# Expert products of a routed feed-forward layer from rounded float32 halves: three products instead of one full float32 product

## The reference

```python
x = x + attention(layernorm(x), W_DKV, W_UK, W_UV, W_UQ, W_O)
xf = layernorm(x).reshape(-1, 256)               # 4096 tokens
topw, topi = top_k(xf @ Wr / temp, 2);  topw = softmax(topw)
for e in range(8):
    a, g = split(xf @ W1[e] + b1[e], 2)          # W1[e]: 256 x 1024
    y = a * silu(g) @ W2[e] + b2[e]              # W2[e]: 512 x 256
    out += y * (weight of expert e for the token, else 0)
x = x + out
```

## Time and profile before

| What | Value |
|---|---|
| median of three runs | 1242.43 us |
| profiled execution, first to last instruction | 1240.9 us |
| PE busy in it | 1069.9 us (86%) |
| DVE, ACT, POOL busy | 787.0, 491.9, 390.4 us |
| projection, attention, routing, expert phase, about | 0 to 126, 126 to 613, 613 to 806, 806 to 1241 us |
| DMA moved | 121.22 MB |

### The profile page before, as it was taken

How to read it: one execution, slowest core, us unless ns; L and a number is a source line. 1 busy time by engine, 2 the same in 40 slices (tenths; PEclk the granted TensorE clock), 3 DMA queues, 4 the chain that set the end, 5 groups by cost and what they waited for, 6 DMA issues and landing times. The chain is left out here.

```text
span 1240.9 us, 19607 instructions
## 1 busy us (share of the span) xinstructions
PE 1069.9 (86%) x5364; PEld 554.3 (45%) x5365; DVE 787.0 (63%) x2352; ACT 491.9 (40%) x1043; POOL 390.4 (31%) x721
## 2 busy tenths in 40 slices
PE   6897599999999999998587553089999999999995
PEld 2443123333333333332176543046666666666663
DVE  5654599999999999894057443245555555555553
ACT  2333047777777777777501212012122122122121
POOL 2224513333333333333403235512222222222222
PEclk9878569999999999999987565589999999999998
DMA  2665974444466644400266641212232232232232
GB/s 91 208 189 188 199 157 104 122 113 113 116 141 135 132 82 79 80 20 30 66 220 193 225 124 68 103 39 44 46 50 42 45 49 42 44 49 42 44 49 25
DMA packets 102396, 121.22 MB, mean 98 GB/s; under 512 B 26352, under 2 KB 81776, under 8 KB 102320
## 3 DMA queue, kind: packets, MB, share of 16 engines
q1 hardware_dynamic: 89024, 102.55, 32.5%
q0 software_dynamic: 13296, 17.77, 8.6%
HBM read 70.27 MB, written 49.63 MB: 97 GB/s over the span
## 5 line engine op out<-in xcount | busy, mean ns | idle before, releaser
L640 ACT ACTIVATE b_prob<-b_prob_ps 128x512 f32<-128x512 f32 (+3 forms) x768 | 318.0, 506 | 103.2 <-PE b_prob_ps L684 101.2
L596 DVE CUSTOM_DVE_ANT_0 b_max_ps<-b_max_ps,b_mask_max 128x384 f32<-128x384 f32 (+3 forms) x512 | 246.7, 503 | 50.4 <-PE b_max_ps L666 47.9
L666 PE MATMUL b_max_ps<-b_k_st,b_q_st 96*128 96x512 bf16 (+3 forms) x768 | 253.5, 345 | 24.2 <-DMA b_k_st<-k_parts 21.8
L684 PE MATMUL b_prob_ps<-b_q_st,b_k_st 99*128 99x512 bf16 (+3 forms) x768 | 239.5, 330 | 10.5 <-ACT b_prob L640 6.6
L554 POOL TENSOR_SCALAR_AFFINE_SELECT b_prob<-b_prob 128x128 f32<-128x128 f32 x512 | 146.6, 292 | 308.6 <-ACT b_prob L640 300.9
L1352 POOL DMA_INDIRECT out_dram<-e_y,e_token x71 | 110.1, 1551 | 326.1 <-DVE e_y L1406 310.4
L599 DVE TENSOR_REDUCE b_neg_max<-b_max_ps 128x1 f32<-128x512 f32 x256 | 176.1, 688 | 5.1 <-PE b_max_ps L666 2.6
L666 PEld LDWEIGHTS b_max_ps<-b_k_st,b_q_st 96*128 96x128 bf16 x768 | 74.4, 99 | 202.0 <-DVE b_neg_max L596 110.1
L703 PE MATMUL b_acc_ps<-b_prob,b_v_aug 128*32 128x512 f32 (+3 forms) x1536 | 163.4, 498 | 0.2 <-POOL b_prob L554 0.2
L1459 PE MATMUL e_g_ps<-w_sb,e_rowsT 128*128 x284 | 135.5, 600 | 0.3 <-issue 0.3
L1459 PE MATMUL e_a_ps<-w_sb,e_rowsT 128*128 x284 | 134.0, 594 | 0.0
(11 more groups left out here) (164 smaller groups left out, 1093.4 us busy)
## 6 DMA issues: line engine op xcount, KB each, us to landing
w_sb<-in_L_ffn_W SPq DMA_DIRECT2D x11, 1024.0 KB, 11.3
e_rows<-slot_rows SPq DMA_DIRECT2D x72, 129.0 KB, 2.1
ctx_cols<-b_ctx_out SPq DMA_DIRECT2D x16, 512.0 KB
q_parts<-a_part_q SPq DMA_DIRECT2D x8, 768.0 KB, 3.8
k_parts<-a_part_k SPq DMA_DIRECT2D x8, 768.0 KB, 4.2
b_q_st<-q_parts SPq DMA_DIRECT2D x16, 384.0 KB, 5.0
b_k_st<-k_parts SPq DMA_DIRECT2D x16, 384.0 KB, 7.7
a_x<-in_L_attn_x SPq DMA_DIRECT2D x8, 512.0 KB, 6.5
```

Source lines behind the costliest of these rows:

```text
L596: nc.vector.tensor_tensor_reduce(scores, scores, mask_max[:, HALF - width:HALF], -1.0, -MASKED, ALU.add, ALU.min, to).then_inc(max_done, 1)
L640: nc.scalar.activation(prob[n % NP][:, 0:width], prob_ps[n % NS][:, 0:width], ACT.Exp, scale=SCALE).then_inc(prob_ok, 1)
L666: nc.tensor.matmul(out[:, 0:width], q_st[g % RING][0:STACK, h, i * P:(i + 1) * P], k_st[g % RING][0:STACK, h, half * HALF:half * HALF + wi ...
L684: nc.tensor.matmul(prob_ps[n % NS][:, 0:width], k_st[g % RING][0:MAXROWS, h, j * P:(j + 1) * P], q_st[g % RING][0:MAXROWS, h, q0:q0 + widt ...
```

## The change

The expert products are no longer made from float32 operands. Each operand is split in two: a high part rounded to the type float32r (float32 words with a shortened mantissa), and a low part, the float32r of the difference. Each product is then three products of float32r operands, high x high, high x low, low x high, summed in PSUM.

*Weights.* In attention SP loads the weights of one expert at a time as they are (`b_w_raw`, 1.5 MB in two DMAs). POOL splits them in 12 pieces of 128 x 256 columns, a cast and a subtraction each, one piece after each of units 24e+8 to 24e+19. In loop step g = 2e+3 SP waits for the last piece of expert e, stores both parts to DRAM (two DMAs of 1.5 MB), and loads the next expert. In routing SP loads the parts of experts 0 to 3 from DRAM into a ring of four experts in SBUF, 3 MB per batch. In the expert phase SP loads expert e over expert e-4 as soon as the last tile of e-4 is done.

*Expert phase.* After each transpose ACT writes the high part, and DVE the low part. The weighting moves from DVE to ACT, the row loads from SP to ACT, the copy of the token numbers from DVE to POOL. B is 6, the loop has six steps, the results of a tile are taken one step later, and the table has one entry more.

The core of the diff:

```diff
-FC_EARLY = 3
+W1_COLS = DC * 2 * FF
+W_COLS = W1_COLS + FC * D
+W_RING = 4
+PIECE = 256
+PIECES = W_COLS // PIECE
...
+    SPLIT_UNITS = TOTAL // EXPERTS
+    SPLIT_FIRST = 8
...
+            def store_split(e):
+                sp.dma_start(dram["w_hi"][e], w_hi[:].bitcast(F32)).then_inc(split_st, 16)
+                sp.dma_start(dram["w_lo"][e], w_lo[:].bitcast(F32)).then_inc(split_st, 16)
...
             load(0)
             for g in range(NQUAD + 2):
                 if g + 1 < NQUAD:
                     load(g + 1)
-                if g < EXPERTS:
-                    sp.dma_start(w1_sb[:, g, :, :], w1[g].rearrange("(c p) n -> p c n", p=P)).then_inc(loaded, 16)
-                elif g < EXPERTS + FC_EARLY:
-                    f = g - EXPERTS
-                    sp.dma_start(w2_early[f][:], w2.rearrange("e (f p) n -> f p e n", p=P)[f]).then_inc(loaded, 16)
+                if g == 0:
+                    load_raw(0)
+                if g >= 3 and g % 2 == 1:
+                    e = (g - 3) // 2
+
+                    sp.wait_ge(lo_ok, PIECES * (e + 1))
+                    store_split(e)
+                    if e + 1 < EXPERTS:
+                        load_raw(e + 1)
                 if 0 <= g - 1 < NQUAD:
                     w = (g - 1) % RING
                     sp.wait_ge(rows_ok, g)
...
+            def split(e, k):
+
+                cols = slice(k * PIECE, (k + 1) * PIECE)
+                if k == 0:
+                    pool.wait_ge(raw_ok, 32 * (e + 1))
+                    if e:
+
+                        pool.wait_ge(split_st, 32 * e)
+                nc.gpsimd.tensor_copy(w_hi[:, cols], w_raw[:, cols]).then_inc(hi_ok, 1)
+                pool.wait_ge(hi_ok, e * PIECES + k + 1)
+                nc.gpsimd.tensor_tensor(w_lo[:, cols], w_raw[:, cols], w_hi[:, cols].bitcast(F32),
+                                        ALU.subtract).then_inc(lo_ok, 1)
...
-                for f in range(FC_EARLY, FC) if b == 0 else ():
-                    sp.dma_start(w2_sb[f][:], w2.rearrange("e (f p) n -> f p e n", p=P)[f]).then_inc(loaded, 16)
+                for part, of in zip(w_ring, (dram["w_hi"], dram["w_lo"])):
+                    sp.dma_start(part[:, b, :].bitcast(F32), of[b]).then_inc(w_in, 16)
...
+            sp.wait_ge(w_in, 32 * W_RING)
+            sp.sem_inc(w_ready, W_RING)
+            for e in range(W_RING, EXPERTS):
+
+                done = sp.value_load(tiles_done[0:1, e - W_RING:e - W_RING + 1], min_val=0, max_val=SLOT_TILES)
+                sp.wait_ge(y_ok, done + B)
+                for part, of in ((w_hi, dram["w_hi"]), (w_lo, dram["w_lo"])):
+                    sp.dma_start(part[:, e % W_RING, :].bitcast(F32), of[e]).then_inc(w_in, 16)
+                sp.wait_ge(w_in, 32 * (e + 1))
+                sp.sem_inc(w_ready, 1)
...
                 pool.wait_ge(y_ok, n + 1 + B)
+                pool.sem_inc(turn, 1)
+                nc.gpsimd.tensor_copy(token[c % B][:], rows[c % B][:, ROW_ID:ROW].bitcast(I32)).then_inc(token_ok, 1)
+                pool.wait_ge(token_ok, n + 1 + B)
                 pool.sem_inc(turn, 1)
                 nc.gpsimd.indirect_dma_start(
...
             def up(n, c, expert):
+                slot = expert % W_RING
+                pe.wait_ge(w_ready, expert + 1)
                 pe.wait_ge(rowsT_ok, n + 1)
...
+                        nc.tensor.matmul(out_ps[:], x_hi[:, chunk], moving(w_hi, slot, at, FF),
+                                         start=(d == 0), stop=False)
+                        nc.tensor.matmul(out_ps[:], x_hi[:, chunk], moving(w_lo, slot, at, FF),
+                                         start=False, stop=False)
+                        last = nc.tensor.matmul(out_ps[:], x_lo[:, chunk], moving(w_hi, slot, at, FF),
+                                                start=False, stop=(d == DC - 1))
```

More of the change, by code:

```diff
@@ L13 @@
 F32 = mybir.dt.float32
+F32R = mybir.dt.float32r
 BF16 = mybir.dt.bfloat16
@@ L556, in _ @@
                                                 channel_multiplier=-1).then_inc(causal_ok, 1)
+                e, k = divmod(unit, SPLIT_UNITS)
+                if SPLIT_FIRST <= k < SPLIT_FIRST + PIECES:
+                    split(e, k - SPLIT_FIRST)
         @block.vector
@@ L1277, in expert_phase @@
         hidden = [sb(f"e_hidden{n}", [P, FF]) for n in range(2)]
-        hiddenT = [sb(f"e_hiddenT{n}", [P, FF]) for n in range(2)]
+        hiddenT = [[sb(f"e_hiddenT_{part}{n}", [P, FF], F32R) for n in range(2)] for part in ("hi", "lo")]
         token = [sb(f"e_token{n}", [P, 1], I32) for n in range(B)]
@@ L1315, in steps @@
                     step(it * U + t, t, None)
-            for n in range(SLOT_TILES, SLOT_TILES + 2):
+            for n in range(SLOT_TILES, SLOT_TILES + tail):
                 step(n, n, n)
@@ L1326, in _ @@
         def _(sp):
-            def load(n, c):
-                row = sp.value_load(tile_row[0:1, n:n + 1] if isinstance(n, int) else tile_row[0:1, bass.ds(n, 1)],
-                                    min_val=0, max_val=EXPERTS * REGION + (SPARE - 1) * P)
-                sp.dma_start(rows[c % B][:], dram["rows"][bass.ds(row, P), :]).then_inc(rows_ok[c % B], 16)
-            for n in range(SLOT_LEAD + 1):
-                if n >= B:
-                    sp.wait_ge(y_ok, n + 1)
-                load(n, n)
-            with sp.Fori(0, LOOPS) as it:
-                for c in range(SLOT_LEAD, SLOT_LEAD + U):
-                    sp.wait_ge(y_ok, it * U + c + 2)
-                    load(it * U + c + 1, c + 1)
+            sp.wait_ge(w_in, 32 * W_RING)
[7 more added lines that the diff above has]
+                sp.sem_inc(w_ready, 1)
         @block.gpsimd
@@ L1424, in silu, with hidden_high, weighted @@
                 nc.scalar.activation(gate[c % 2][:], g_sum[c % 2][:], ACT.Silu).then_inc(gate_ok, 1)
-            def hidden_turned(n, c):
+            def hidden_high(n, c):
                 act.wait_ge(hiddenT_ps_ok, n + 1)
-                nc.scalar.activation(hiddenT[c % 2][:], hiddenT_ps[:], ACT.Copy).then_inc(hiddenT_ok, 1)
-            def step(n, c, value):
+                if not isinstance(n, int) or n >= 2:
+                    act.wait_ge(y_ps_ok, n - 1)
+                nc.scalar.activation(hiddenT[0][c % 2][:], hiddenT_ps[:], ACT.Copy).then_inc(hiddenT_hi_ok, 1)
+            def weighted(n, c):
+                act.wait_ge(y_sum_ok, n + 1)
+                nc.scalar.activation(y[c % B][:], y[c % B][:], ACT.Copy,
+                                     scale=rows[c % B][:, ROW_W:ROW_W + 1]).then_inc(y_ok, 1)
+            def step(n, c, value):
+                if value is None or 2 <= n < SLOT_TILES + 2:
+                    hidden_high(n - 2, c - 2)
+                if value is None or n + 1 < SLOT_TILES:
+                    rows_high(n + 1, c + 1)
+                if value is None or 3 <= n < SLOT_TILES + 3:
+                    weighted(n - 3, c - 3)
+                if value is None or n + AHEAD < TABLE:
+                    load(n + AHEAD, c + AHEAD)
                 if value is None or n < SLOT_TILES:
                     silu(n, c)
-                if value is None or 1 <= n <= SLOT_TILES:
-                    hidden_turned(n - 1, c - 1)
-            steps(act, step)
+            for n in range(AHEAD):
+                load(n, n)
+            rows_high(0, 0)
+            steps(act, step, 3)
+            for n in range(SLOT_TILES, TABLE):
+                act.wait_ge(rows_ok[n % B], (n // B + 1) * 16)
         @block.tensor
@@ L1507, in build @@
     project_phase(nc, dram, x, w_dkv, w_uk, w_uv, w_uq)
-    with ExitStack() as ctx:
-        w1_sb = ctx.enter_context(nc.sbuf_tensor("w1_sb", [P, EXPERTS, DC, 2 * FF], F32))
-        w2_early = [ctx.enter_context(nc.sbuf_tensor(f"w2_sb{f}", [P, EXPERTS, D], F32)) for f in range(FC_EARLY)]
-        loaded = ctx.enter_context(nc.semaphore("loaded"))
-        attention_phase(nc, dram, w1, w1_sb, w2, w2_early, loaded)
-        mixed_phase(nc, dram, x, w_o, w_r, temp, (b1, b2), w2, w1_sb, w2_early, loaded, out)
+    attention_phase(nc, dram, w1, w2)
+    mixed_phase(nc, dram, x, w_o, w_r, temp, (b1, b2), out)
 _INS = ["L0_attn_x", "L0_attn_W_DKV", "L0_attn_W_UK", "L0_attn_W_UV", "L0_attn_W_UQ", "L0_attn_W_O", "L0_ffn_Wr",
```

143 lines of the change are left out of this document (95 added, 48 removed).

## The result

The changed kernel takes 1300.3 us (median of four runs, 1297.5 to 1305.7), beside 1243.2 us for the kernel before: ratio 1.047, 95% interval 1.042 to 1.052, slower: 57 us more. The forecast was 1288 us, 46 us more than before. The profiled execution has a span of 1303.2 us, 62.3 more than before.

| phase (from, to) | before | after | difference | forecast |
|---|---|---|---|---|
| projection (start to SP's first stack load) | 126.4 | 132.2 | +5.8 | 0 |
| attention (to routing's first load) | 487.8 | 560.1 | +72.3 | +70 |
| routing (to the start of the last group of pad stores) | 165.0 | 165.9 | +0.9 | +8 |
| from there to the first add | 49.3 | 49.6 | +0.3 | +3 |
| first to last add, 70 intervals | 404.8 | 387.9 | -16.9 | -35 |

What follows compares the result with a forecast made beforehand. PE was taken to bound the kernel, busy 86% of the span. From 1240.9 us, +70 attention, +8 routing and -32 expert phase gave 1287 us, 1288 as median; range 1218 to 1345.

Steps and rivals of the forecast that it cites:

- seven stalls of 8 + 2 us: Attention: PE waits 8 us for row maxima queued behind SP's bulk, then loses 2 us to a slow clock; +70 us.
- Rival B: Attention: the small DMAs are not held up, costing at most 10 us there; 1222 us in all, faster; chance 16%.
- POOL's splits: Attention: 96 splits at 1.1 us each, 106 us in all on POOL, barely fit; cost 0, at most 10 us.
- Rival D: Attention: POOL can't keep up, splits take 2 us instead of 1.1; 1323 us in all; chance 6%.
- One stream of 512 columns: Expert phase, PE: a float32r product streams its columns once, 0.215 us, making a tile 4.6 us instead of 5.8.
- Rival C: Expert phase: a float32r product costs a whole record, 8.4 us per tile; 1527 us in all; chance 6%.
- POOL's cycle: Expert phase: POOL's add, landing and token copy take 5.0 us, more than PE's 4.6, and set the pace; 55 us gained.
- The extra step of the pipeline: Expert phase: one step more of pipeline before the first add costs 3 us.
- Reloads: Expert phase: four reloads of 3.1 MB beside adds and row loads cost 5 us each, 20 us; bounds nothing to 41 us.
- Routing: DVE's residual waits longer for a store behind more bytes: 6 us in batch 1, 2 us later; +8 us (3 to 25).

## Why the prediction was right, step by step

**Attention, right in mechanism and size.** Forecast was seven stalls of 8 + 2 us. Measured are seven waits of 7.2 to 8.5 us, 7.8 in the mean (54.6 / 7), and 72.3 - 54.6 = 17.7 us more, 2.5 per stall, in which the slower clock and the few us of splits and traffic are contained. The undoing of the order alone gives 68.7 us back. The reason that I gave was too narrow, though: I argued from `c_temp` on one queue that order within the queue holds the small DMAs. On a queue of their own they still take 7.5 us. The Trainium skill (DMA: Bandwidth & Descriptors, "Queues, rings and completion order") says that engines take descriptors in ring order; by ring order alone separate queues would have freed them, and the runs show that this is 2.3 of the 8 us. The same section says that the queues of SP and ACT are rings on the same 16 DMA engines; with that the 7.5 us agree. How these engines divide their time between two queues no run here shows. Rival B fell either way.

**POOL's splits, right.** They cost 0.40 + 0.73 us, 1.16 us from the cast's start to the start of what follows, against 1.1 forecast, and stay hidden. Rival D fell.

**float32r, right in kind, 7% off in size.** One stream of 512 columns takes 0.23 us where I took 0.215; PE's tile is 4.9 us where I had 4.6. The 0.66 us that I carried over for transposes is now 0.75 too. It did not show in the total, since POOL's cycle is longer still, but it halves what a faster POOL can bring. Rival C fell. The Trainium skill (FP8 and Floating Point Precision, "TensorE Precision Notes") counts four passes for true float32; a quarter of its 0.86 us here is 0.215 us, and the trace agrees with that within 7%.

**POOL's cycle, right as the bound, small in size.** The median interval is 5.13 us instead of 5.0: 70 x 0.13 = 9 us. The 5.0 were 4.63, the distance of two adds at the end of the kernel before, + 0.21 for the copy + 0.15 for its wait. The copy takes 0.19 us; so the term that was mis-sized is the wait, which adds 5.13 - 4.63 - 0.19 = 0.3 us, just above the bound of 0.28 that I gave. The 0.83 us that the trace has between copy and DMA are not this term. A part of them stood in the 4.63 already, as idleness behind the landing:

```profile
1228.64 1.55 POOL L1352 DMA_INDIRECT out_dram<-e_y,e_token  x1 [3.08 <-DMA out_dram<-e_y,e_token]
```

Before, 3.08 us lie between the end of one DMA's start and the next DMA; with the change 2.47 us lie between it and the copy, and the other 0.6 us stand, as it seems, behind the copy now. The extra step of the pipeline cost 0.3 us instead of 3.

**Reloads, mis-sized.** 20 us forecast, 27 to 28 measured by leaving them out, inside the bounds of 0 to 41. Next to each reload one interval of adds is 9.5 to 11.7 us, and the row loads land late as well.

**Routing, not confirmed on the first chip, too small on the second.** +8 forecast, +0.9 and +11.9 measured. I had put 2 us on the later batches, because the store lands long before DVE comes to it. On the second chip DVE waits there too, 2.1 and 8.9 us.

**Projection.** The 5.8 us are not the change's. The kernel before needs 126.4 us in one trace and 131.7 in the other, and the changed ones lie near either value.

The sum: 1287 + 5.8 (projection) + 2.3 (attention) - 7.1 (routing) - 2.7 (extra step) + 18.1 (adds) - 0.1 (end) = 1303.3 us. It must come out, since the phases make up the span. Of the 18.1 us, 9 are POOL's cycle and 7 the reloads; 2 are not accounted for. Part of the total's accuracy is luck: routing and the extra step, too dear in the forecast by 9.8 us together, cover half of what the adds had too little. On the second chip routing does not help, and the change costs 1275.0 - 1205.1 = 70 us, where 46 were forecast and 57 measured on the first.

## What to carry to other kernels

Start a bulk transfer that is off the critical path right after the small transfers on which an engine is about to wait, not right before; moving either to another queue brought the landing forward by a little over a quarter of the delay and the phase nothing, moving it in time gave 68.7 of the 72.3 us back. When a product gets cheaper, work out the serial cycle of whoever is next (here POOL's add, its landing, and anything put between the two), and let nothing else into it. Cut reloads that have slack into pieces that land one after the other.

## What the runs showed of the hardware

- Three DMAs of 8 KB take 1.8 us alone, 9.8 us behind 4.7 MB on their queue, and 7.5 us beside the same 4.7 MB on another queue.
- With the bulk under way, starting three small DMAs takes SP 3.7 instead of 1.8 us, and ACT 3.4 us.
- From the end of POOL's copy of the token numbers to the start of the indirect DMA that reads them, semaphore steps included, it is 0.80 to 0.84 us.
- Beside a reload of 3.1 MB one accumulating indirect DMA takes 8.2 to 10.4 us to land, where 3.8 is usual.
- The same program takes 165.0 us in the routing phase on one chip and 123.4 on another (kernel before), with attention and adds equal to 0.3 us; its projection takes 126.4 us in the one run and 131.7 in the other.
